# V's high part behind the exponential on ScalarE, V's low part behind the probabilities' low part on VectorE, at steps 4 to 7 of a head

## The reference

```python
q = proj(Wq, bq) * scale; k = proj(Wk, bk); v = proj(Wv, bv)   # x is (4, 1024, 256)
q = apply_rotary(pos, q); k = apply_rotary(pos, k)
sim = jnp.einsum('bhid,bhjd->bhij', q, k)
sim = jnp.where(causal, -jnp.finfo(sim.dtype).max, sim)
attn = jax.nn.softmax(sim, axis=-1)
out = jnp.einsum('bhij,bhjd->bhid', attn, v)
out = out.transpose(0, 2, 1, 3).reshape(b, n, INNER) @ Wo + bo
x = layernorm(x + out)
x = layernorm(x + ffn(x))   # silu(x @ Wg * sg) * (x @ Wu * su), then @ Wd * sd
```

## Time and profile before

| | |
|---|---|
| median of 3 runs | 2173.8 us (2173.39 to 2177.66) |
| the profiled execution's own time | 2175.21 us |
| its span, first to last instruction | 2173.4 us |
| granted TensorE clock, mean | 0.988 |
| busy: TensorE, VectorE | 2089.3 us (96%), 1750.5 us (81%) |
| busy: ScalarE, GpSimd | 1416.5 us (65%), 1304.1 us (60%) |

### The profile page before, as it was taken

How to read it: one execution, slowest core, us unless ns; L and a number is a source line. 1 busy time by engine, 2 the same in 40 slices (tenths; PEclk the granted TensorE clock), 3 DMA queues, 4 the chain that set the end, 5 groups by cost and what they waited for, 6 DMA issues and landing times. The chain is left out here.

```text
span 2173.4 us, 49354 instructions
## 1 busy us (share of the span) xinstructions
PE 2089.3 (96%) x13136; PEld 1860.5 (86%) x13136; DVE 1750.5 (81%) x3547; ACT 1416.5 (65%) x3230; POOL 1304.1 (60%) x1080
## 2 busy tenths in 40 slices
PE   6999999999999999999999999999999999979997
PEld 5888888888888888888888888888888888868886
DVE  5788888888888888888888888888888888865776
ACT  4676666676666666666667666676666776654543
POOL 4566656676666666576666666675666666524554
PEclk8999999999999999999999999999999999988999
DMA  4432223233232332333222233323232223310000
GB/s 115 148 73 68 72 73 73 64 86 75 73 73 73 67 69 70 73 92 70 68 68 73 73 73 70 84 72 73 74 69 68 68 73 73 80 25 1 29 19 29
DMA packets 99871, 150.27 MB, mean 69 GB/s; under 512 B 31216, under 2 KB 35824, under 8 KB 99312
## 3 DMA queue, kind: packets, MB, share of 16 engines
q1 hardware_dynamic: 85856, 115.82, 22.2%
q10 hardware_dynamic: 13968, 33.95, 5.7%
HBM read 78.15 MB, written 4.46 MB: 38 GB/s over the span
## 5 line engine op out<-in xcount | busy, mean ns | idle before, releaser
L582 DVE TENSOR_TENSOR PT<-TP,PT 128x512 fp32r<-128x512 f32 (+3 forms) x768 | 421.3, 552 | 210.0 <-ACT PT L402 206.7
L527 ACT ACTIVATE prob<-prob,neg_max 128x128 f32<-128x128 f32 (+7 forms) x512 | 397.8, 777 | 288.4 <-DVE neg_max L670 280.4
L402 ACT ACTIVATE PT<-TP 128x512 fp32r<-128x512 f32 (+3 forms) x768 | 361.4, 489 | 90.3 <-PE TP L833 80.6
L670 DVE CUSTOM_DVE_ANT_0 prob<-S,mask_row 128x128 f32<-128x128 f32 (+7 forms) x512 | 380.7, 744 | 27.1 <-PE TP L833 12.4
L347 POOL TENSOR_TENSOR swap<-swap,sin_t 128x512 f32<-128x512 f32 x256 | 350.3, 1368 | 82.7 <-DMA swap<-proj 80.4
L833 PE MATMUL TP<-ident,prob 128*128 128x128 f32 x2304 | 369.4, 274 | 0.7 <-ACT prob L527 0.7
L833 PEld LDWEIGHTS TP<-ident,prob 128*128 128x128 f32 x2304 | 283.1, 141 | 55.5 <-ACT prob L527 1.1
L646 DVE TENSOR_TENSOR rot<-rot,swap 128x512 f32<-128x512 f32 x256 | 286.3, 1119 | 7.6 <-POOL swap L347 7.2
L358 POOL TENSOR_TENSOR QKB<-rot,QKB 128x512 fp32r<-128x512 f32 x128 | 171.8, 1342 | 196.1 <-ACT QKB L402 196.1
L358 POOL TENSOR_TENSOR QKA<-rot,QKA 128x512 fp32r<-128x512 f32 x128 | 182.4, 1425 | 169.1 <-ACT QKA L402 168.4
L823 PE MATMUL S<-QKB 128*128 128x512 f32 (+4 forms) x1152 | 261.2, 353 | 1.3 <-DVE resid L692 1.3
(11 more groups left out here) (107 smaller groups left out, 4722.9 us busy)
## 6 DMA issues: line engine op xcount, KB each, us to landing
swap<-proj SPq DMA_DIRECT2D x512, 128.0 KB, 2.3
recip_b<-recip_d SPq DMA_DIRECT2D x128, 256.0 KB, 3.6
w_raw<-in_w_heads ACTq DMA_DIRECT2D x65, 384.0 KB, 3.1
wo_raw<-in_wo_heads ACTq DMA_DIRECT2D x32, 256.0 KB, 3.3
resid<-in_x_rows SPq DMA_DIRECT2D x4, 1024.0 KB, 11.3
out<-resid SPq DMA_DIRECT2D x8, 512.0 KB, 3.0
x_raw<-in_x_cols SPq DMA_DIRECT2D x3, 1024.0 KB, 5.2
recip_d<-recip SPq DMA_DIRECT2D x128, 2.0 KB, 1.8
```

Source lines behind the costliest of these rows:

```text
L402: copy = lambda o, i: nc.scalar.activation(o, i, ACT.Copy)
L527: nc.scalar.activation(row, row, ACT.Exp, bias=neg_max[:, s:s + 1], scale=-1.0, accum_out=row_sum[:, s:s + 1]).then_inc(exped, 1)
L582: sub = lambda o, a, b: nc.vector.tensor_tensor(o, a, b, ALU.subtract)
L670: nc.vector.tensor_tensor_reduce(row_view(prob[g][:, prob_at[g][i]:prob_at[g][i] + cols], s), score_view(S[s % 2], s), row_view(mask_row[: ...
```

## The change

The change moves one block of code on ScalarE and one on VectorE. At steps 4 to 7 ScalarE now first copies the high part of a piece of probabilities and takes the exponential of the step, and then copies V's high part. VectorE first makes the probabilities' low part and then V's two operations. TensorE's, GpSimd's and SyncE's lists are the same; so are all waits and all instructions.

```diff
@@ ScalarE, steps 4 to 7
+                    if s >= 4 and own:
+                        probs_hi(n, s + 4)
+                    if own and s >= 4:
+                        softmax(n, s)
                     if s >= 4 and project:
                         v = s - 4
                         act.wait_ge(v_made, n_four(m, v))
                         wait(act, attended, n_step(n, 7))
                         copy(V[nxt][:, 0, 2 * v:2 * v + 2, :],
                              v_psum[:, :, 0, :]).then_inc(v_hi, 1)
-                    if s >= 4 and own:
-                        probs_hi(n, s + 4)
-                    if own and s >= 4:
-                        softmax(n, s)
@@ VectorE, steps 4 to 7
+                    if s >= 4 and own:
+                        probs_lo(n, s + 4)
                     if s >= 4 and project:
                         v = s - 4
                         dve.wait_ge(v_hi, n_four(m, v))
...
                         dve.wait_ge(v_sub, n_four(m, v))
                         nc.vector.tensor_tensor(V[nxt][:, 1, tiles, :], v_rest[:, :, :], v_psum[:, :, 1, :],
                                                 ALU.add).then_inc(v_lo, 1)
-                    if s >= 4 and own:
-                        probs_lo(n, s + 4)
```

## The result

The changed kernel takes 2444.16 us, the median of 4 runs (2442.85 to 2444.9); before is 2175.73 on the same chip (4 runs, 2173.39 to 2178.39). The ratio is 1.1233, 95% interval 1.1213 to 1.1252: slower by 12.3%. The forecast was 2454 us.

The account below looks back on a forecast made before the run. TensorE bounds the kernel, the other engines just in time (cushion 0.24 us at V's pair). Waits of 63 x (1.56 + 0.84 + 1.99) = 277, + 12, - 9 give 280 us more: 2454 us, range 2375 to 2510.

Parts of the forecast that it names:

- V's copy behind the exponential: Step 4: V's copy starts at 1003.24 instead of 1001.49, so TensorE waits 1.56 us for step 5's pair.
- The loop: Steps 5 to 7, ScalarE and VectorE: pairs 3.80, then 3.98 us apart against TensorE's 2.96; waits 0.84 and 1.02.
- rival of one wait a head: Only step 5 waits, 1.56 us, and steps 6 and 7 find V ready: 2272 us; chance 0.08.
- that of no loss: Rival: V's low part still arrives before the next pair and old waits shrink, 2126 us at best; chance 0.02.
- GpSimd in the way: Step 5: L358 starts ahead of the rotation's addition and lengthens it by 0.97 us; step 7's wait becomes 1.99.
- The clock: Rival: the waits make TensorE's clock fall, 1.7 us a time; 2490 us in a third of heads, 2561 in all; chance 0.24.
- The signs: What the trace would show: L878 waits near 280 us, three a head, heads about 33.8 and 34.3 us, clock 1.00.
- The sum: Whole program: 63 x (1.56 + 0.84 + 1.99) = 277, + 12, - 9 = 280 us added.
- second term: Wait at step 6, pair 1 to pair 2: 3.80 us apart against TensorE's 2.96, so 0.84 us a head.
- The head's start: Even heads: first probabilities' low part late by some 0.45 us (0 to 0.9); a wait of 0.4, 12 us in all.
- the 9 us that I took off: Existing waits at L878, 17.3 us: about half, before head 0, stays; 9 us are subtracted.
- Its old wait at step 4: Odd head, TensorE's wait for the probabilities' low part at L848, from step 3's tail: claimed to stay.

Follow-up runs that it names:

- e5: The changed kernel, but on ScalarE V's copy stands between the probabilities' copy and the exponential; 2226.31 us, ratio 1.0247.
- e2: VectorE's list as in the changed kernel, ScalarE's as in the kernel before; 2268.11 us, ratio 1.0438.
- e4: The changed kernel, but at step 5 VectorE makes the rotation's addition ahead of V's two operations; 2352.52 us, ratio 1.0829.
- e3: The changed kernel, but at step 5 ScalarE copies Q's or K's high part ahead of the probabilities' copy; 2387.05 us, ratio 1.0989.
- e1: ScalarE's list as in the changed kernel, VectorE's as in the kernel before; 2599.47 us, ratio 1.1965.

## Why the prediction was right

- *V's copy behind the exponential.* Predicted 2.17 from exponential to pair (0.82 + 1.35), measured 2.15 (1072.31 to 1074.46). e5 shows that the exponential makes the waits of steps 6 and 7. Of the 1.54 at step 5 it makes 0.48; the other 1.06 is there without it, behind VectorE's half (e2, e5). The prediction had the sum of that path right and did not see this second one, which the exponential's path hides.
- *The loop.* Predicted pairs 3.80 and 4.95 us apart (3.98 + 0.97), measured 3.79 and 4.88. e4 and e5 break it in two places, and the time follows; the rival of one wait a head (2272) and that of no loss (2126) are out.
- *GpSimd in the way.* Predicted 0.97 more on the rotation's addition, measured 1.60 - 0.68 = 0.92; e3 takes 57 us off where I had 61. The rule of the Trainium skill (SBUF — State Buffer, Who interferes with whom) reached further than the rows did, and the trace agrees: L358 holds the addition up when it starts first and leaves it alone when it starts later.
- *The clock.* The rival (2490 to 2561) did not come about: idle times of 1.30, 0.47 and 1.68 us in a head leave it at 1.00, with three short stretches in 63 heads. e1, with 1.31, 2.00 and up to 1.68, has 60 of them, so the doubt was well placed; which of e1's waits brings them on was not tried. Even there they cost some 10 us and not the 1.7 us a time that the rival put on them.
- *The signs.* The waits at L878 were to rise to some 280 us, near 1.6, 0.8 and 2.0 in a head. The profile has 226.5 us, at 1.30, 0.47 and 1.68. The spacings of the pairs, which is what the prediction added up, give 1.54, 0.74 and 1.92: the profile counts the rest as busy time of TensorE.
- *The sum.* Predicted 280 us for the profiled execution, measured 2441.9 - 2173.4 = 268.5 in span. It is this close in part by luck, since terms of 10 us and more were off in both directions. At the pairs I had 4.39 a head, and even heads show 1.54 + 0.74 + 1.92 = 4.20, so 63 x 0.19 = 12 us too much. TensorE's own work from pair 1 to pair 2 is 3.03 us, not the 2.96 of the later step, which is most of the second term's error. A row of the kernel before, to set against 1003.03 in the earlier trace rows:

```profile
1006.06 0.36 PE L878 MATMUL PJ<-WB,xT 128*128 128x256 f32 x1
```

The head's start cost more than the 0.4 I gave it: an even head is 34.17 - 29.06 = 5.11 longer, of which 4.20 lie at the pairs and 0.9 is left for the start, which is the bound I had named (31 x 0.5 = 15 us too little). The odd head gave that back. By the median it took 3.59 us from pair 1 to pair 2 before, and takes 3.78 now, so the new wait takes the place of the old one and adds 0.19 where the sum counted 0.84; the 9 us that I took off cover half of that, and the forecast of 34.3 for an odd head took it into account where the sum did not (30.36 + 4.39 is 34.75). Its old wait at step 4 shrank by 0.16 as well, where I had said that it stays. The heads came out at 34.17 and 34.09 where I had 33.8 and 34.3.

## What to carry to other kernels

Before work is put behind something in an engine's list, ask what the thing that it now waits for waits for itself: here a single swap on ScalarE closed a loop (exponential, copy, subtraction, addition, rotation, mask) whose 3.8 to 4.9 us replaced TensorE's 3.0 as the pace. Add up the loop from rows of the trace before; it came out within 0.1 us. When e1 moved one operation, the loop had to be added up again with GpSimd in it: left out, it cost 0.93 us a head. And look at who starts first on VectorE and GpSimd: the order of starts, not their amount of work, decides a microsecond.

## What the runs showed of the hardware

- VectorE's addition of two SBUF tiles (L646, 2816 of them in the eleven traces) took 0.68 or 0.69 us in all 1478 cases in which no GpSimd operation ran at its start, also where one started during it. Where a GpSimd operation had started 0.04 us or more ahead, it ended 0.54 to 0.66 us after that operation's end, in all 1205 cases, and took up to 1.81 us.
- Waits of TensorE of 1.68 us once a head left the granted clock at 1.00 but for three stretches of 3.4 us; with waits of 1.31, 2.00 and up to 1.68 us in a head (e1) its mean fell to 0.953, about one such stretch a head.
- Two moves that cost 427 us (e1) and 96 us (e2) alone cost 268 us together.
